# Eight subtractions of expert weights, six of them on GpSimd and two on VectorE, all placed on VectorE behind the early list

## Chip, cores and metric

The kernel runs on one core of one Trainium2 chip. The metric is the device time of one execution in microseconds (us); lower is better.

## What is computed

A layer of attention without a score matrix, a norm, a layer of experts and a second norm, on 4 sequences of 1024 tokens with 512 features, in fp32. The parts that matter here:

```python
x_prev = shift x by one token
k, v, r = (x_prev + (x - x_prev) * tm) @ W.T + b        # three mixes, three matrices
wkv = _wkv_scan(k, v, time_decay, time_first)           # running maximum, two weighted sums, their quotient
out = (sigmoid(r) * wkv) @ Wo.T + bo
x = _layernorm(x + out)
logits = xt @ wg
probs = softmax(logits); idx = argmax(probs)            # one expert of 8 for each token
expert_out = xt @ W[e].T + b[e]                         # only the chosen one counts
x = _layernorm(x + gate * expert_out)
```

## The kernel before

Products of fp32 operands are made of fp32r parts: each operand is rounded to a high part, and the remainder is the low part; a product is high x high + high x low + low x high. For the weights of the experts ScalarE rounds (`expert_hi`, line 957, into `w_e_hi`), and the low part `w_e_lo` is the subtraction `w_e_raw - w_e_hi`, written over the raw weights. Each of the 8 experts is 4 pieces of 128x512.

The work has two stages. The first goes over 8 blocks (4 sequences, 2 halves of 512 tokens), each in 4 chunks of 128 features: TensorE projects k, v and r (line 511), VectorE runs the recurrence (three scans and their products), GpSimd adds the entering state to the sums (`leave`, lines 1093 and 1095), ScalarE does exponentials. The output projection (line 529), the first norm and the logits of a block follow one or two blocks later. The rows go to `x1_rows` in HBM.

The second stage is the experts. Tokens are sorted by expert, in tiles of 128 rows. Of the first 24 row tiles an early list is made while the last block is still under way; from it come 17 full tiles (`FULL`), each of one expert. The rest, with the last 8 row tiles, makes 22 mixed tiles. For each tile GpSimd gathers rows by an indirect DMA (`gather`, line 1174), TensorE turns them (line 680) and multiplies (`expert`, line 689), VectorE adds bias and residual (lines 1719 and 1726), ScalarE normalizes (`norm2`, lines 1041 to 1047), and GpSimd scatters the rows to the output (line 1181). Six tiles are in flight.

The order of each engine is written out by hand; engines meet by semaphores alone. On VectorE, behind the last block's recurrence, stand in this order: the rows of the block before (`add_rows`, line 1319, with `statistics`, line 1329, and `aggregate`, line 1333), the columns of the early list (`early_columns`, lines 1574 to 1579), their split (`split_dest`), the matrices of tiles and slots (`place_tiles`, lines 1506 and 1508, `place_slots`, line 1501), the experts of the full tiles (`tile_experts`, lines 1512 to 1519, with `tiles_ready`), the first row tile of the last block (`add_last` and `shift_last`, lines 1524 to 1531), the ids (line 1643, with `ids_ready`), and the other three row tiles, with the subtractions of experts 6 and 7 (line 1539) between them. TensorE multiplies the slot and tile matrices into the list (`list_full`, line 662, `listed`).

On GpSimd, `expert_lo` (line 1157) subtracts experts 0 to 5 in four pieces each; it stands ahead of the first gather, and expert 0 ahead of the last chunk's `leave`. The counter `we_split` is raised once for each expert, in the order of the experts:

```python
part.then_inc(we_split, 1)                       # GpSimd, experts 0 to 5
dve.wait_ge(we_split, e)                         # VectorE, experts 6 and 7: in order behind GpSimd's
pe.wait_ge(we_split, e + 1)                      # TensorE, ahead of a full tile of expert e
pe.wait_ge(we_split, EXPERTS)                    # TensorE, ahead of the mixed tiles
pool.wait_ge(ids_ready, 1)                       # GpSimd, ahead of the first gather
pool.wait_ge(gate_stored[0], 16)
pe.wait_ge(turned_lo, k + 1)                     # TensorE, ahead of tile k: VectorE's split_gathered(k)
pe.wait_ge(y_taken, k + (TILES + 1))             # and VectorE's additions up to add_gathered(k - 2)
```

Of the kernel before, what the change touches and what calls it, by code (L numbers as in the profile page):

```python
# [31 lines left out]
ALU = mybir.AluOpType  # L32
ACT = mybir.ActivationFunctionType
AX_X = mybir.AxisListType.X
F32 = mybir.dt.float32
# [26 lines left out]
PART = 8  # L62
BIAS_RING = 3
AHEAD = 5
POOL_EXPERTS = 6
ROW = H + 16
EPS = 1e-5
EXPONENT_CAP = 27.0
# [35 lines left out]
def build(nc, x, xT, w_square, w_experts, vectors, bo, b_experts, wg, out):  # L104
    x1_rows = nc.dram_tensor("x1_rows", [TOKENS + 1, ROW], F32, kind="Internal").ap()

    with ExitStack() as ctx:
# [251 lines left out]
        def home(e):  # L359

            return (e + EXPERTS - 2) % EXPERTS
# [718 lines left out]
        def _(pool):  # L1080
# [6 lines left out]
            def leave(i, c):  # L1087

                g = i * CH + c
                p, b = c // 2, c % 2  # L1090
                pool.wait_ge(b_scanned, g + 1)
                pool.wait_ge(evn_ready, g + 1)
                pool.tensor_tensor(ee[:, p, b, :], ee[:, p, b, :], state[:, b, SB, 0:TB], ALU.add).then_inc(den_added, 1)  # L1093
                pool.wait_ge(a_scanned, g + 1)
                pool.tensor_tensor(evn[:, p, b, :], evn[:, p, b, :], state[:, b, SA, 0:TB], ALU.add).then_inc(num_added, 1)
# [54 lines left out]
            walk(pool, step, pool.Fori)  # L1150


            def expert_lo(e):
                pool.wait_ge(we_hi, e + 1)
                p = home(e)
                for c in range(CH):
                    part = pool.tensor_tensor(w_e_lo[:, p, c], w_e_raw[:, p, c], w_e_hi[:, p, c].bitcast(F32), ALU.subtract)  # L1157
                part.then_inc(we_split, 1)

            last = BLOCKS - 1  # L1160
            mix_lo(last, R, 0)
            mix_lo(last, R, 1)
            for c in range(CH - 1):
                leave(last, c)
            expert_lo(0)
            leave(last, CH - 1)
            for e in range(1, POOL_EXPERTS):
                expert_lo(e)

            def gather(k):  # L1170
                if k >= RING:
# [38 lines left out]
        def _(dve):  # L1210
# [310 lines left out]
            def add_last(j):  # L1521
                dve.wait_ge(last_loaded, TPB * 16)
                dve.wait_ge(y_filled, last * TPB + (j + 1))
                dve.tensor_tensor(rows_last[:, j], rows_last[:, j], last_banks[j], ALU.add).then_inc(y_taken, 1)
                dve.wait_ge(y_taken, last * TPB + (j + 3))
                dve.bn_stats(bn[:, j, :], rows_last[:, j]).then_inc(bn_done, 1)
                aggregate(last, j)
# [6 lines left out]
            def expert_lo(e):  # L1534

                p = home(e)
                dve.wait_ge(we_split, e)
                dve.wait_ge(we_hi, e + 1)
                dve.tensor_tensor(w_e_lo[:, p], w_e_raw[:, p], w_e_hi[:, p].bitcast(F32), ALU.subtract).then_inc(we_split, 1)

# [92 lines left out]
            place_tiles(place_k, 0, EARLY, COLS)  # L1633
            for n in range(EARLY // PART):
                place_slots(place_early[n], n * PART, PART)
            tile_experts(FULL, taken[:, 1:], iota_row, after_full, expert_full, slot_full)
            link(dve.tensor_tensor(left_end[:], ranked[:, 1, :], taken[:], ALU.subtract))
            link(dve.tensor_tensor(n_left[:], counts[:, 0, 1:], n_taken[:], ALU.subtract))
            add_last(0)
            shift_last(0)  # L1640
            dve.wait_ge(listed, 1)
            dve.tensor_copy(left_row[:], lists_ps[:, FULL:FULL + LEFT])
            dve.tensor_scalar(ids_full[:, :, 0], lists_ps[:, 0:FULL], -1.0, None, ALU.add).then_inc(ids_ready, 1)
            add_last(1)
            shift_last(1)
            expert_lo(6)
            add_last(2)
            shift_last(2)

            def choose_late():  # L1650
                largest(EARLY, LATE, late_ps, lg2)
# [91 lines left out]
            split_gathered(0, 0)  # L1743
            add_last(3)
            split_gathered(1, 1)
            shift_last(3)
            expert_lo(7)
            add_bias(0, 0, 0)
            add_bias(1, 0, 1)
# [76 lines left out]
```

## Time and profile before

| | |
|---|---|
| median of 3 runs | 684.97 us |
| the runs | 684.97, 684.98, 683.03 us |
| the profiled execution | 683.71 us |
| its span | 681.7 us |
| mean granted TensorE clock | 0.947 of full speed |
| VectorE busy | 565.0 us |
| TensorE busy | 591.1 us |
| GpSimd busy | 319.4 us |

The time of a run covers a little more than the span, which goes from the first to the last instruction of the profiled execution: 2.0 us here. Times below are counted from the span's start. PE is TensorE, DVE is VectorE, ACT is ScalarE, POOL is GpSimd, SPq the queue of SyncE's transfers. In brackets stands how long the engine was idle before the instruction and what ended the wait.

### The profile page before, as it was taken

Reading aid. Unit: us, or ns where it says so; the run is one execution under the profiler, and the core shown is the slowest. Engines: PE = TensorE matmul, PEld = TensorE weight load, DVE = VectorE, ACT = ScalarE, POOL = GpSimd, SP = SyncE. Lnnn points to the kernel's source line nnn. Section 1 sums busy time; section 2 is a strip of 40 time slices with the busy share of each in tenths; the row PEclk is TensorE's granted clock in tenths of the full one; section 3 lists DMA queues with packets and bytes.
Section 4 is the critical chain, followed back from the end, with each engine's and each line's share of the span. In section 5 each row is a group of like instructions: output and inputs, shape, how many; then the busy total and the mean of one; then the engine's idle time right before and its main releaser. Section 6 shows DMA issues by size and latency. Waiting matters only on the chain. (4 is left out here: it accounts for less than half of the span.)

```text
span 681.7 us, 8970 instructions
## 1 busy us (share of the span) xinstructions
PE 591.1 (87%) x2484; PEld 435.7 (64%) x2485; DVE 565.0 (83%) x873; ACT 403.0 (59%) x735; POOL 319.4 (47%) x237
## 2 busy tenths in 40 slices
PE   0676779999999999999999999987669779899992
PEld 0464666676677777668668668743448657677771
DVE  7959898999999999999999899799866658576661
ACT  3356475487477567766756756543446446587763
POOL 4744545444443551552462453276841435456541
PEclk9779898999999999999999999898779879899996
DMA  8030010032032022003104106246153566757650
GB/s 306 5 123 1 0 62 0 1 108 63 15 104 67 16 78 76 31 32 122 31 4 151 32 0 232 91 171 197 62 187 80 159 189 188 206 178 220 210 163 6
DMA packets 36565, 67.63 MB, mean 99 GB/s; under 512 B 8560, under 2 KB 8560, under 8 KB 36532
## 3 DMA queue, kind: packets, MB, share of 16 engines
q1 hardware_dynamic: 30292, 48.29, 22.5%
q0 software_dynamic: 6240, 18.94, 8.8%
q8 instruction: 16, 0.26, 0.2%
q14 instruction: 17, 0.14, 0.1%
HBM read 50.17 MB, written 18.88 MB: 101 GB/s over the span
## 5 line engine op out<-in xcount | busy, mean ns | idle before, releaser
L1083 POOL TENSOR_TENSOR mixed<-unsplit,mixed 128x1024 fp32r<-128x1024 f32 x44 | 104.4, 2395 | 133.8 <-ACT mixed L762 133.8
L511 PE MATMUL kb<-mixed,w_kvr 128*128 128x512 f32 x384 | 99.6, 410 | 23.8 <-DVE mixed L1437 16.9
L689 PE MATMUL y_ps<-w_e_hi,xgT 128*128 x312 | 111.0, 418 | 7.3 <-issue 5.2
L511 PE MATMUL vb<-mixed,w_kvr 128*128 128x512 f32 x384 | 102.8, 419 | 14.4 <-DVE evn L1275 8.9
L511 PE MATMUL rb<-mixed,w_kvr 128*128 128x512 f32 x384 | 101.8, 415 | 5.7 <-DVE ee L1289 4.7
L511 PEld LDWEIGHTS kb<-mixed,w_kvr 128*128 128x128 f32 x384 | 74.7, 198 | 42.6 <-issue 16.5
L529 PE MATMUL y_ps<-w_o,rw 128*128 128x512 f32 x224 | 100.7, 592 | 0.0
L511 PEld LDWEIGHTS vb<-mixed,w_kvr 128*128 128x128 f32 x384 | 74.5, 198 | 36.1 <-DVE evn L1275 11.7
L511 PEld LDWEIGHTS rb<-mixed,w_kvr 128*128 128x128 f32 x384 | 73.4, 193 | 27.8 <-DVE ee L1289 5.9
L1226 DVE SCALAR_TENSOR_TENSOR unsplit<-diff,vec,xb 128x512 f32<-128x512 f32 x96 | 74.2, 833 | 8.1 <-PE kb L511 6.1
L1093 POOL TENSOR_TENSOR ee<-ee,state 128x512 f32<-128x512 f32 x32 | 34.9, 1092 | 96.2 <-DVE state L1259 95.5
L689 PEld LDWEIGHTS y_ps<-w_e_hi,xgT 128*128 128x128 f32 x312 | 61.2, 196 | 24.3 <-issue 11.3
L529 PEld LDWEIGHTS y_ps<-w_o,rw 128*128 128x128 f32 x224 | 42.5, 190 | 42.3 <-issue 40.4
L777 ACT ACTIVATE e<-state 128x512 f32<-128x512 f32 x32 | 20.2, 630 | 75.6 <-DVE state L1243 75.6
L689 PE MATMUL y_ps<-w_e_lo,xgT 128*128 x156 | 63.6, 408 | 0.0
L762 ACT ACTIVATE mixed<-unsplit 128x1024 fp32r<-128x1024 f32 x48 | 50.5, 1054 | 19.2 <-DVE unsplit L1226 19.2
L1726 DVE SCALAR_TENSOR_TENSOR yo<-y_ps,xg,yo 128x512 f32<-128x512 f32 x39 | 29.2, 750 | 35.6 <-PE y_ps L689 21.9
L1157 POOL TENSOR_TENSOR w_e_lo<-w_e_raw,w_e_hi 128x512 fp32r<-128x512 f32 x24 | 38.0, 1614 | 14.1 <-ACT w_e_hi L957 14.1
L1181 POOL DMA_INDIRECT out<-yo,ids_full x17 | 18.1, 1065 | 49.7 <-ACT yo L1047 27.5
L1259 DVE TENSOR_TENSOR_SCAN state<-eb,state,e 128x512 f32<-128x512 f32 x32 | 40.8, 1274 | 0.4 <-ACT state L812 0.4
L1047 ACT ACTIVATE yo<-yo,nmr,rstd 128x512 f32<-128x512 f32 x39 | 31.8, 816 | 15.2 <-DVE nmr L1733 12.2
L1236 DVE TENSOR_TENSOR_SCAN state<-kb,state,wdec 128x512 f32<-128x512 f32 x32 | 40.3, 1259 | 0.0
(227 smaller groups left out, 1104.6 us busy)
## 6 DMA issues: line engine op xcount, KB each, us to landing
bias<-b_experts SPq DMA_DIRECT2D x39, 256.0 KB
w_e_raw<-w_experts SPq DMA_DIRECT2D x8, 1024.0 KB, 8.2
rows<-x SPq DMA_DIRECT2D x28, 256.0 KB, 2.6
x_rows<-rows SPq DMA_DIRECT2D x28, 256.0 KB, 2.1
xb<-xT SPq DMA_DIRECT2D x4, 1026.0 KB, 5.3
xb<-xT SPq DMA_DIRECT2D x3, 1024.0 KB, 5.1
w_raw<-w_square SPq DMA_DIRECT2D x2, 1024.0 KB, 10.4
xb<-xT SPq DMA_DIRECT2D x2, 512.0 KB, 5.3
```

Source lines behind the costliest of these rows:

```text
L511: mm = pe.matmul(bank, w_kvr[m][:, a, h, o:o + P], mixed[m][:, bb, h, :], start=(k == 0), stop=(k == 3 * CH - 1))
L529: mm = pe.matmul(y_ps[:, j % 2, :], rw[:, half, c, j * P:(j + 1) * P], w_o[:, c, :], start=False, stop=(c == CH - 1))
L689: mm = pe.matmul(y_ps[:, n % 2, :], xgT[n % 3][:, a, c, :], w[:, bass.ds(p, 1), c, :].rearrange("p u o -> p (u o)"), start=(c == 0 and (a, ...
L762: act.activation(mixed[m][:, HI, 2 * hp:2 * hp + 2, :], unsplit[m][:, LO, 2 * hp:2 * hp + 2, :], ACT.Copy).then_inc(mixed_hi, 1)
L1047: act.activation(yo[n][:], yo[n][:], ACT.Identity, bias=nmr2[:, n:n + 1], scale=rstd2[:, n:n + 1]).then_inc(out_ready, 1)
L1083: pool.tensor_tensor(mixed[m][:, LO, 2 * hp:2 * hp + 2, :], unsplit[m][:, LO, 2 * hp:2 * hp + 2, :], mixed[m][:, HI, 2 * hp:2 * hp + 2, :] ...
L1093: pool.tensor_tensor(ee[:, p, b, :], ee[:, p, b, :], state[:, b, SB, 0:TB], ALU.add).then_inc(den_added, 1)
L1157: part = pool.tensor_tensor(w_e_lo[:, p, c], w_e_raw[:, p, c], w_e_hi[:, p, c].bitcast(F32), ALU.subtract)
L1226: ins = dve.scalar_tensor_tensor(out=unsplit[m][:, LO, h, :], in0=diff[:, h, :], scalar=vec[:, VEC_MK + m, h:h + 1], in1=xb[:, h, 0:TB], o ...
L1236: dve.tensor_tensor_scan(state[:, c % 2, SQ, 1:], kb[:], wdec[:, c:c + 1].to_broadcast([P, TB]), state[:, c % 2, SQ, 0:1], ALU.max, ALU.ad ...
L1259: dve.tensor_tensor_scan(state[:, c % 2, SB, 1:], eb[:], e2[:, c % 2], state[:, c % 2, SB, 0:1], ALU.mult, ALU.add).then_inc(b_scanned, 1)
L1726: dve.scalar_tensor_tensor(out=yo[n][:], in0=y_ps[:, n % 2, :], scalar=gate_of(n), in1=yo[n][:], op0=ALU.mult, op1=ALU.add, accum_out=sum2 ...
```

## The change

GpSimd subtracts no expert any more. VectorE subtracts all eight, each in one operation on 128x2048, and no longer waits for the counter of the expert before. Expert 0 stands ahead of the ids, behind the first row tile; experts 1 to 4 between and behind the row tiles 1 and 2; experts 5 to 7 around the fourth row tile. The operations of `tile_experts` move from ahead of the first row tile to behind the ids.

```diff
--- before.py
+++ after.py
@@ -62,7 +62,6 @@
 PART = 8
 BIAS_RING = 3
 AHEAD = 5
-POOL_EXPERTS = 6
 ROW = H + 16
 EPS = 1e-5
 EXPONENT_CAP = 27.0
@@ -1150,22 +1149,11 @@
             walk(pool, step, pool.Fori)
 
 
-            def expert_lo(e):
-                pool.wait_ge(we_hi, e + 1)
-                p = home(e)
-                for c in range(CH):
-                    part = pool.tensor_tensor(w_e_lo[:, p, c], w_e_raw[:, p, c], w_e_hi[:, p, c].bitcast(F32), ALU.subtract)
-                part.then_inc(we_split, 1)
-
             last = BLOCKS - 1
             mix_lo(last, R, 0)
             mix_lo(last, R, 1)
-            for c in range(CH - 1):
+            for c in range(CH):
                 leave(last, c)
-            expert_lo(0)
-            leave(last, CH - 1)
-            for e in range(1, POOL_EXPERTS):
-                expert_lo(e)
 
             def gather(k):
                 if k >= RING:
@@ -1534,7 +1522,6 @@
             def expert_lo(e):
 
                 p = home(e)
-                dve.wait_ge(we_split, e)
                 dve.wait_ge(we_hi, e + 1)
                 dve.tensor_tensor(w_e_lo[:, p], w_e_raw[:, p], w_e_hi[:, p].bitcast(F32), ALU.subtract).then_inc(we_split, 1)
 
@@ -1633,19 +1620,23 @@
             place_tiles(place_k, 0, EARLY, COLS)
             for n in range(EARLY // PART):
                 place_slots(place_early[n], n * PART, PART)
-            tile_experts(FULL, taken[:, 1:], iota_row, after_full, expert_full, slot_full)
+            add_last(0)
+            shift_last(0)
+            expert_lo(0)
             link(dve.tensor_tensor(left_end[:], ranked[:, 1, :], taken[:], ALU.subtract))
             link(dve.tensor_tensor(n_left[:], counts[:, 0, 1:], n_taken[:], ALU.subtract))
-            add_last(0)
-            shift_last(0)
             dve.wait_ge(listed, 1)
             dve.tensor_copy(left_row[:], lists_ps[:, FULL:FULL + LEFT])
             dve.tensor_scalar(ids_full[:, :, 0], lists_ps[:, 0:FULL], -1.0, None, ALU.add).then_inc(ids_ready, 1)
+            tile_experts(FULL, taken[:, 1:], iota_row, after_full, expert_full, slot_full)
             add_last(1)
+            expert_lo(1)
             shift_last(1)
-            expert_lo(6)
             add_last(2)
+            expert_lo(2)
             shift_last(2)
+            expert_lo(3)
+            expert_lo(4)
 
             def choose_late():
                 largest(EARLY, LATE, late_ps, lg2)
@@ -1743,7 +1734,9 @@
             split_gathered(0, 0)
             add_last(3)
             split_gathered(1, 1)
+            expert_lo(5)
             shift_last(3)
+            expert_lo(6)
             expert_lo(7)
             add_bias(0, 0, 0)
             add_bias(1, 0, 1)
```

VectorE from the slot matrices to the ids; before, from the fourth of the seven operations of `tile_experts` on (`place_early` are the slot matrices, `rows_last` the last block's row tiles, `ids_full` the list that the gathers read):

```order
L1515 TENSOR_SCALAR moved_e<-tile_e 128x17
L1516 SCALAR_TENSOR_TENSOR moved_e<-tile_e,moved_e 128x17
L1518 CAST expert_full<-tile_e 128x17
L1519 CAST slot_full<-moved_e 128x17
L1637 TENSOR_TENSOR left_end<-ranked,taken 128x9
L1638 TENSOR_TENSOR n_left<-counts,n_taken 128x8
L1524 TENSOR_TENSOR rows_last<-rows_last,rb 128x512
L1526 BN_STATS bn<-rows_last 128x6
L1333 BN_AGGR stats<-bn 128x2
L1531 SCALAR_TENSOR_TENSOR nmr<-stats,rstd 128x1
L1642 COPY left_row<-lists_ps 128x14
L1643 TENSOR_SCALAR ids_full<-lists_ps 128x17
```

and in the change, from the last slot matrix on:

```order
L1489 TENSOR_TENSOR place_early_127<-slot_q,iota_q 128x1024
L1512 TENSOR_TENSOR rows_last<-rows_last,rb 128x512
L1514 BN_STATS bn<-rows_last 128x6
L1321 BN_AGGR stats<-bn 128x2
L1519 SCALAR_TENSOR_TENSOR nmr<-stats,rstd 128x1
L1526 TENSOR_TENSOR w_e_lo<-w_e_raw,w_e_hi 128x2048
L1626 TENSOR_TENSOR left_end<-ranked,taken 128x9
L1627 TENSOR_TENSOR n_left<-counts,n_taken 128x8
L1629 COPY left_row<-lists_ps 128x14
L1630 TENSOR_SCALAR ids_full<-lists_ps 128x17
L1500 TENSOR_TENSOR after_full<-iota_row,taken 128x136
```

The seven operations from `after_full` to `slot_full` no longer stand between the slots and the ids; a subtraction of `w_e_lo` does.

VectorE from the second row tile (`rows_last<-rows_last,vb`) to the splits of the gathered tiles 0 and 1 (`xgT`), before:

```order
L1524 TENSOR_TENSOR rows_last<-rows_last,vb 128x512
L1526 BN_STATS bn<-rows_last 128x6
L1333 BN_AGGR stats<-bn 128x2
L1531 SCALAR_TENSOR_TENSOR nmr<-stats,rstd 128x1
L1539 TENSOR_TENSOR w_e_lo<-w_e_raw,w_e_hi 128x2048
L1524 TENSOR_TENSOR rows_last<-rows_last,y_ps 128x512
L1526 BN_STATS bn<-rows_last 128x6
L1333 BN_AGGR stats<-bn 128x2
L1531 SCALAR_TENSOR_TENSOR nmr<-stats,rstd 128x1
L1710 TENSOR_TENSOR xgT_129<-kb,xgT_129 128x512
L1524 TENSOR_TENSOR rows_last<-rows_last,y_ps 128x512
```

and in the change:

```order
L1512 TENSOR_TENSOR rows_last<-rows_last,vb 128x512
L1514 BN_STATS bn<-rows_last 128x6
L1321 BN_AGGR stats<-bn 128x2
L1526 TENSOR_TENSOR w_e_lo<-w_e_raw,w_e_hi 128x2048
L1519 SCALAR_TENSOR_TENSOR nmr<-stats,rstd 128x1
L1512 TENSOR_TENSOR rows_last<-rows_last,y_ps 128x512
L1514 BN_STATS bn<-rows_last 128x6
L1321 BN_AGGR stats<-bn 128x2
L1526 TENSOR_TENSOR w_e_lo<-w_e_raw,w_e_hi 128x2048
L1519 SCALAR_TENSOR_TENSOR nmr<-stats,rstd 128x1
L1526 TENSOR_TENSOR w_e_lo<-w_e_raw,w_e_hi 128x2048 x2
L1701 TENSOR_TENSOR xgT_129<-kb,xgT_129 128x512
```

One subtraction (expert 6) stood between the second row tile and the split of tile 0; four stand there now (experts 1 to 4).

GpSimd from the last chunks of the recurrence (`ee`, `evn`) to the first gathers, before:

```order
L1157 TENSOR_TENSOR w_e_lo<-w_e_raw,w_e_hi 128x512 x4
L1093 TENSOR_TENSOR ee<-ee,state 128x512
L1095 TENSOR_TENSOR evn<-evn,state 128x512
L1157 TENSOR_TENSOR w_e_lo<-w_e_raw,w_e_hi 128x512 x20
L1174 DMA xg<-x_rows,ids_full 128x528 x6
```

and in the change:

```order
L1092 TENSOR_TENSOR ee<-ee,state 128x512
L1094 TENSOR_TENSOR evn<-evn,state 128x512
L1092 TENSOR_TENSOR ee<-ee,state 128x512
L1094 TENSOR_TENSOR evn<-evn,state 128x512
L1162 DMA xg<-x_rows,ids_full 128x528 x6
```

Nothing stands between the last `leave` and the gathers any more.

## Rows read from the trace of the kernel before

**Rows 1.** The page: busy time of each engine with its share of the span.

```profile
PE 591.1 (87%) x2484; PEld 435.7 (64%) x2485; DVE 565.0 (83%) x873; ACT 403.0 (59%) x735; POOL 319.4 (47%) x237
```

**Rows 2.** Timeline of GpSimd (POOL), 440 to 535 us: start, length, engine, line, operation.

```profile
463.08 11.70 POOL L1157 TENSOR_TENSOR w_e_lo<-w_e_raw,w_e_hi 128x512 fp32r<-128x512 f32 x8 [4.93 <-ACT w_e_hi L957]
479.67 14.35 POOL L1157 TENSOR_TENSOR w_e_lo<-w_e_raw,w_e_hi 128x512 fp32r<-128x512 f32 x8 [4.89 <-ACT w_e_hi L957]
497.84 1.15 POOL L1174 DMA_INDIRECT xg<-x_rows,ids_full  x1 [3.82 <-DVE ids_full L1643]
...
500.56 2.32 POOL L1174 DMA_INDIRECT xg<-x_rows,ids_full  x1 [0.30 <-issue]
...
526.74 0.98 POOL L1174 DMA_INDIRECT xg<-x_rows,ids_full  x1 [0.30 <-issue]
```

**Rows 3.** Timeline of VectorE, 454 to 502 us.

```profile
454.55 1.19 DVE L1560 TENSOR_SCALAR counts_i<-counts_i 128x18 int32<-128x18 int32 x1
...
462.50 1.23 DVE L1302 SCALAR_TENSOR_TENSOR er<-ee,er 128x1024 f32<-128x1024 f32 x1
463.76 2.18 DVE L1312 SCALAR_TENSOR_TENSOR rw<-evn,er 128x1024 f32<-128x1024 f32 x1
...
469.71 1.26 DVE L1574 TENSOR_TENSOR beyond<-work_early,n_taken 128x192 f32<-128x192 f32 x1
...
473.69 1.30 DVE L1577 TENSOR_TENSOR work_early<-work_early,beyond 128x192 f32<-128x192 f32 x1
475.03 0.36 DVE L1578 TENSOR_TENSOR work_early<-work_early,hot_early 128x192 f32<-128x192 f32 x1
...
480.12 0.83 DVE L1324 SCALAR_TENSOR_TENSOR nmr<-stats,rstd 128x2 f32<-128x2 f32 x1 [2.94 <-ACT rstd L840]
...
481.85 1.91 DVE L1508 TENSOR_TENSOR place_k<-place_k,token 128x768 fp32r<-128x768 f32 x1
...
490.32 1.35 DVE L1512 TENSOR_TENSOR after_full<-iota_row,taken 128x136 f32<-128x136 f32 x1
...
494.99 0.69 DVE L1524 TENSOR_TENSOR rows_last<-rows_last,rb 128x512 f32<-128x512 f32 x1
...
497.38 0.17 DVE L1643 TENSOR_SCALAR ids_full<-lists_ps 128x17 uint32<-128x17 f32 x1
...
499.76 2.29 DVE L1539 TENSOR_TENSOR w_e_lo<-w_e_raw,w_e_hi 128x2048 fp32r<-128x2048 f32 x1
```

**Rows 4.** Line 1501 by form: shortest, median, longest ns, first and last start.

```profile
L1501 DVE TENSOR_TENSOR place_early<-slot_q,iota_q x3: 2284/2289/2293, 483.7 to 488.1; 128x1024 fp32r<-128x1024 f32 x3
L1501 DVE TENSOR_TENSOR place_late<-slot_q,iota_q x1: 1216/1216/1216, 562.9 to 562.9; 128x1024 fp32r<-128x1024 f32 x1
```

**Rows 5.** Busy time of engines, granted clock, DMA share and GB/s in three stretches.

```profile
440.00:497.00 57.00, 41.92 (x131) 23.97 (x129) 51.96 (x72) 24.83 (x30) 40.29 (x26) 0.88 0.44 149
533.80:538.30 4.50, 4.47 (x14) 3.56 (x14) 1.01 (x3) 1.61 (x6) 1.50 (x2) 0.62 0.50 165
538.80:541.70 2.90, 2.90 (x16) 2.31 (x14) 2.73 (x9) 1.80 (x5) 0.00 (x0) 1.00 0.35 95
```

**Rows 6.** Timeline of TensorE, 455 to 535 us.

```profile
459.68 0.47 PE L517 MATMUL y_ps<-bo,ones 128*128 128x512 f32 x1 [1.03 <-DVE rows L1319]
459.98 3.60 PE L529 MATMUL y_ps<-w_o,rw 128*128 128x512 f32 x8
...
511.45 0.50 PE L689 MATMUL y_ps<-w_e_hi,xgT 128*128 x1 [1.28 <-issue]
...
521.43 0.47 PE L689 MATMUL y_ps<-w_e_hi,xgT 128*128 x1
...
531.96 0.66 PE L680 MATMUL kb<-ident,xg 128*128 128x128 f32 x4 [2.53 <-DMA xg<-x_rows,ids_full]
```

**Rows 7.** Timeline of ScalarE, 477 us.

```profile
477.70 1.89 ACT L957 ACTIVATE w_e_hi<-w_e_raw 128x2048 fp32r<-128x2048 f32 x1
```

**Rows 8.** Timeline of the SyncE queue, 477 us: its transfers.

```profile
477.11 5.75 SPq L393 DMA_DIRECT2D x_rows<-rows  x4
```

## Prediction

> **What bounds the kernel now.** I read the page first: VectorE is busy 83% of the span and TensorE 87% [rows 1], means over stages with different limits. The chain that ended last shows only the closing transfer, so the bound near the change has to be read from the timelines of 440 to 535 us, engine by engine, GpSimd's first. It holds 24 list subtractions (four to an expert, experts 0 to 5); the last ended at 479.67 + 14.35 = 494.02, and the first gather of rows starts at 497.84, behind the write of `ids_full` by VectorE, which ends at 497.55 [rows 2, 3]. So GpSimd was not late. What its work costs is seen on VectorE: with GpSimd in a subtraction, an operation on 128x192 takes 1.30 us; GpSimd stops at 463.08 + 11.70 = 474.78, and the next one of the same size takes 0.36 [rows 2, 3]. An 18-element operation takes 1.19; a 1024-element product takes 2.18 where the refinement of the same size before it, with GpSimd idle, took 1.23; the three slot matrices take 2.29 each, the same form alone 1.22 [rows 3, 4]. And VectorE has no slack there: it is busy for 52.0 of the 57 us from 440 to 497 [rows 5]. VectorE sets the time of the list, and GpSimd slows VectorE: that is what the change touches.
>
> From the ids to the first expert tile it is TensorE that sets the time now, working in order through logits, the last output projection and turned rows; tile 0 starts at 511.45, tile 2 at 521.43 [rows 6].
>
> **The change, part by part.** All times are places in the profiled execution; I follow the same chain through the new order.
>
> *1. GpSimd's pieces are gone, up to the end of the slots.* Before 466 us the relief is partly lost. The refinement and the product at 442 to 447 would give back 1.0 each, but the gate behind them waits for ScalarE, and some 0.3 is left. Four 1.19 us operations of the counts fall to about 0.2 (4 us), the product at 463.76 from 2.18 to 1.23; TensorE binds instead. The last projection of the block before starts at 459.68 behind a wait of 1.03 us for VectorE and ends at 459.98 + 3.60 = 463.58 [rows 6]; without that wait and 0.3 earlier it ends at 462.3. One addition, four statistics and four aggregates follow (3.3 us at 0.6, 0.6 and 0.08 each, none of them slowed now): the columns of the list start at 465.6 and not at 469.71 [rows 3]. **Gain 4.1.**
> The columns: four operations of 1.30 fall to 0.36, **3.8.** Then VectorE waits 2.94 us for ScalarE's deviation, which stands behind a rounding of 1.89 [rows 3, 7]. ScalarE's inputs come earlier by the same 7.9 us, so I keep the wait. Behind it the shift falls from 0.83 to 0.16, the tile product from 1.91 to 0.95 (three quarters of the 1.22 form), and the slot matrices from a pitch of 2.2 to 1.14 (their length less the 0.08 by which such operations overlap): **4.8.** The slots are complete 12.7 us earlier, at 477.7; TensorE's listing ends 2 us behind them and hides behind the next item.
>
> *2. The order up to the ids.* Now 7.2 us lie between slots and ids (490.32 to 497.55): seven operations of the tile numbers and two small ones to 494.99, row tile 0 with its shift, the ids [rows 3]. Then: row tile and shift 2.4, one subtraction 2.2 (2.29 less the overlap), the two small ones 0.4, the ids 0.3, together 5.3; the tile numbers come behind. **Gain 2.0** after rounding. The ids are ready at 482.8, 14.7 earlier. The gathers also need the stored rows of the block before; those stores start at 477.11 [rows 8] behind ScalarE's norm, so they move up by 4 to 8 us and don't bind.
>
> *3. From the ids to tile 0.* Now 511.45 - 497.55 = 13.9 us, set by TensorE. Then VectorE is the long way: tile numbers 1.6 (seven at some 0.2, GpSimd idle), row tile 1 1.6, subtraction 1 2.2, a shift 0.1, row tile 2 1.6, subtraction 2 2.2, a shift 0.1, subtractions 3 and 4 4.4, and only then the split of gathered tile 0, 0.7: 14.5 us, to 497.3. TensorE turns tile 2 (0.6), passes the gap of 1.28 that stands there now [rows 6] and starts tile 0 at 499.2, 16.4 us behind the ids. **Loss 2.4**, so tile 0 is 12.3 us earlier. TensorE's own way, through the norm of row tile 2, brings it to the turns by about 495.4, so it is covered. Of the other subtractions none is waited for: number 5 ends at 501.5, 6 and 7 at 506; the addition behind them, which tile 2 needs, ends at 508.6, and tile 2 is due at 509.2 (521.43 - 511.45 behind tile 0). That cover is 0.6 us thin.
>
> *4. TensorE's clock.* The granted clock is 0.62 from 533.80 to 538.30, the tile behind a wait of 2.53 us for a gather, and 1.00 in the next; the two take 4.5 and 2.9 us [rows 5, 6]. Tile 0 now comes right behind the last projection and the turns, and is fast. In the new order TensorE idles some two us before turn 2, and more before that, so I take a slow tile 0: **loss 1.6.** Bounds: nothing if the clock is up, 3.2 if two tiles are slow.
>
> *5. Behind tile 2* I move the stage rigidly. The first scatter hangs on TensorE's turns of the last rows and ScalarE behind them, gather 6 (526.74) on that scatter, and turn 6 waits for it at 531.96 [rows 2, 6]. The loop has the same members in the same order in both kernels.
>
> Sum: 4.1 + 3.8 + 4.8 + 2.0 - 2.4 - 1.6 = 10.7 us. The profiled execution took 683.71 (span 681.7 and 2.0 around it), which gives 673.0. The median of the runs shown is 684.97, 1.26 above that execution, with one run of three below it; I add half a microsecond: **673.5.**
>
> The relief's bounds: 0, if the operations keep their length, and about 18, if every slowed one of the stretch counted. I take 12.7, since rows of equal shape beside each other carry it and only what others bind is taken off.
>
> **The rivals.**
> *A, the forecast:* a gain of 8.5 to 13 (675.2 to 670.7). For it: equal shapes at 1.30 and 0.36 us with only GpSimd's stop between them.
> *B, more:* the clock is up and VectorE gets to the split as early as the ids allow: the whole 14.7 reaches the end, 669.0. Against it: four subtractions stand ahead of the split in VectorE's order.
> *C, gathers and subtractions collide.* The six gathers now start at 483 and fall on subtractions 1 and 2. In the kernel before the third gather takes 2.32 us where the one at 526.74 takes 0.98; it starts 0.8 us into the subtraction at 499.76 [rows 2, 3]. A late gather costs nothing: three times 1.4 more puts the start of the sixth at 494, and with 5.2 us to landing (526.74 to 531.96) it is there ahead of its tile. But if the gather goes first and VectorE stands for it, six times 0.98 = 5.9 lie on the long way of item 3, and 4.8 of the gain is left: 678.9. Against: the subtraction at 499.76 beside the gathers kept its 2.29.
> The Trainium skill, SBUF — State Buffer, section "Who interferes with whom", says that a tensor operation on two tensors has no two-port mode and takes only the shared read interface, from which it infers that it does not hold up descriptor generation on GpSimd; by that page C would not occur and its chance would go to A. The 2.32 us gather speaks against that inference, so I keep C.
> *D, slower:* the relief does not come, because the long VectorE operations are due to the transfers of the weights or the rows and not to GpSimd. Then item 2's 2.0 us stand against 2.4 + 1.6 of items 3 and 4, in front of tile 0: 2.0 us slower, 685.7. It decides from a relief below 2.0 us, where I count 12.7. Against it: 1.22 for the form at 562.9 and 0.36 at 475.03 [rows 3, 4]. That the change doesn't do what it says is no case: the order of both engines shows it.
>
> **How the numbers follow.** A 0.60; B 0.15; C and other partial losses, a gain of 2 to 8.5 us, 0.18; an end within 0.3% (2 us), about what a measurement of this kernel can tell from no change, 0.03; D 0.04. The low end is B less half a microsecond, 668.5; the high end is C, 679.0. Faster 0.93, same 0.03, slower 0.04.
>
> **What would show it.** Right: slot matrices of 1.2 us, column operations near 0.36, the write of the ids near 482.7 and GpSimd's first gather 0.3 behind it; VectorE without a gap from there to the split of tile 0 near 497; tile 0 near 499 at a granted clock of about 0.6, tile 2 near 510.5; and from tile 2 to the end 160 us as now. Wrong: slot matrices still above 2 us (D); subtractions 1 and 2 longer than 3 us (C); tile 0 before 498 or at full clock (B); or a distance from tile 2 to the end that differs by over 2 us, which none of the items holds.

## The result, and the profile after

The changed kernel takes 665.79 us (median of 4 runs, 664.97 to 667.01), the kernel before in the same session 684.98 (683.03 to 685.92). The ratio is 0.9725, 95% interval 0.9699 to 0.9751: 19 us, 2.8% faster. The forecast was 673.5 with a range down to 668.5; the direction was right, and the gain is two thirds larger than forecast and outside the range.

The profiled execution took 664.97 us with a span of 663.0, against 683.71 and 681.7: 18.7 us less. Span and busy times on the page of the changed kernel (before: [rows 1]):

```profile
span 663.0 us, 8951 instructions
...
PE 583.5 (88%) x2484; PEld 431.0 (65%) x2485; DVE 559.8 (84%) x879; ACT 403.1 (61%) x735; POOL 281.2 (42%) x213
```

VectorE does 13.6 us more subtraction and is busy 5.2 us less, so its other operations are 18.8 us shorter together. Where the 18.7 us lie is read by comparing the same instructions. VectorE, from the columns of the list to the first addition of the experts (answers to [rows 3]):

```profile
464.93 0.32 DVE L1561 TENSOR_TENSOR beyond<-work_early,n_taken 128x192 f32<-128x192 f32 x1
...
466.07 0.36 DVE L1564 TENSOR_TENSOR work_early<-work_early,beyond 128x192 f32<-128x192 f32 x1
...
466.47 0.36 DVE L1565 TENSOR_TENSOR work_early<-work_early,hot_early 128x192 f32<-128x192 f32 x1
...
471.55 0.16 DVE L1312 SCALAR_TENSOR_TENSOR nmr<-stats,rstd 128x2 f32<-128x2 f32 x1 [2.94 <-ACT rstd L839]
...
473.49 3.49 DVE L1489 TENSOR_TENSOR place_early<-slot_q,iota_q 128x1024 fp32r<-128x1024 f32 x3
...
481.88 0.17 DVE L1630 TENSOR_SCALAR ids_full<-lists_ps 128x17 uint32<-128x17 f32 x1
...
495.56 0.68 DVE L1701 TENSOR_TENSOR xgT<-kb,xgT 128x512 fp32r<-128x512 f32 x1
...
506.88 0.74 DVE L1717 SCALAR_TENSOR_TENSOR yo<-y_ps,xg,yo 128x512 f32<-128x512 f32 x1
```

The column operation at 466.07 takes 0.36 as the one behind it (before 1.30 and 0.36); the three slot matrices take 3.49 together and not 6.71; the ids are written at 481.88, 15.5 us earlier than 497.38. TensorE, the starts of tiles 0, 1 and 2 and the turn of tile 6 (answers to [rows 6]):

```profile
498.26 0.79 PE L688 MATMUL y_ps<-w_e_hi,xgT 128*128 x1 [0.78 <-issue]
...
504.03 0.48 PE L688 MATMUL y_ps<-w_e_hi,xgT 128*128 x1
...
509.88 0.47 PE L688 MATMUL y_ps<-w_e_hi,xgT 128*128 x1
...
519.08 0.66 PE L679 MATMUL kb<-ident,xg 128*128 128x128 f32 x4 [1.20 <-DMA xg<-x_rows,ids_full]
```

Tile 2 starts 11.55 us earlier than at 521.43. From there to the end of the span it is 153.1 us where it was 160.3: **7.1 us of the gain lie behind tile 2**, where I had moved everything rigidly. GpSimd, two of the first six gathers, the first scatter and gather 6 (answers to [rows 2]):

```profile
486.30 1.90 POOL L1162 DMA_INDIRECT xg<-x_rows,ids_full  x1 [0.30 <-issue]
...
489.76 2.24 POOL L1162 DMA_INDIRECT xg<-x_rows,ids_full  x1 [0.30 <-issue]
...
513.55 1.03 POOL L1169 DMA_INDIRECT out<-yo,ids_full  x1 [21.55 <-ACT yo L1046]
...
514.88 0.98 POOL L1162 DMA_INDIRECT xg<-x_rows,ids_full  x1 [0.30 <-issue]
```

| step of the forecast | forecast | measured |
|---|---|---|
| 0: anything ahead of 440 us | 0 | 0.5 |
| 1: start of the columns | 4.1 | 4.3 (469.71 to 464.93, less 0.5) |
| 1: columns | 3.8 | 3.8 |
| 1: shift, tile and slot matrices | 4.8 | 4.9 (slots complete at 476.89, before 490.32) |
| 2: slots to ids | 2.0 | 2.1 (5.2 us, before 7.2) |
| 3: ids to tile 0 | -2.4 | -2.3 (16.2 us, before 13.9) |
| 4: slow clock in tile 0 | -1.6 | -1.6 (tile 0 to 1: 5.77, before 4.13) |
| 5: tile 2 to the end | 0 | 7.1 |

(The difference of the sum to 18.7 is rounding.) The start of every tile of the second stage, from TensorE's timelines of both kernels (first product of each), shows where the 7.1 us arise:

```
tile           before            after       earlier by
2              521.43            509.88      11.6
3              526.39  +4.96     514.84 +4.96   11.6
4              533.83  +7.44     520.80 +5.96   13.0
5              538.82  +4.99     524.86 +4.06   14.0
8              553.67  +8.37     536.84 +5.52   16.8
9              558.91  +5.24     541.37 +4.53   17.5
12             570.92  +4.68     551.93 +3.24   19.0
17             591.29  +5.97     572.77 +5.79   18.5
36             659.72            641.08         18.6
```

(+ is the distance from the tile before.) TensorE turns the rows of gather 6 ahead of tile 4 and those of gather 10 ahead of tile 8, where it waited 3.42 us before and 0.61 now. So the delays go round with the ring: 2.4 us are gained at tiles 4 and 5, 3.5 at 8 and 9, 1.5 up to 12, and 0.4 is lost later. Tile 4 of the kernel before ran at a granted clock of 0.62 [rows 5]; now:

```profile
521.00:524.00 3.00, 3.00 (x16) 2.46 (x16) 1.00 (x4) 1.53 (x5) 0.85 (x2) 1.00 0.80 269
```

The granted clock (behind the busy times) is 1.00. TensorE waited 1.20 us for gather 6, before 2.53 [rows 6].

### The profile page after: what moved, and what is told of

It is laid out like the page before. It is cut to its first block and busy times, and to the rows that moved or that the text cites. A ratio compares the mean times of both kernels' runs of the same rounds, so it can differ in the third digit from the quotient of the medians.

```text
span 663.0 us, 8951 instructions
## 1 busy us (share of the span) xinstructions
PE 583.5 (88%) x2484; PEld 431.0 (65%) x2485; DVE 559.8 (84%) x879; ACT 403.1 (61%) x735; POOL 281.2 (42%) x213
## 5 line engine op out<-in xcount | busy, mean ns | idle before, releaser
L688 PE MATMUL y_ps<-w_e_hi,xgT 128*128 x312 | 109.6, 414 | 7.8 <-issue 6.0
L510 PEld LDWEIGHTS kb<-mixed,w_kvr 128*128 128x128 f32 x384 | 73.9, 196 | 44.1 <-issue 16.2
L1254 DVE TENSOR_TENSOR_SCAN state<-eb,state,ev 128x512 f32<-128x512 f32 x32 | 40.3, 1258 | 0.0
L1094 POOL TENSOR_TENSOR evn<-evn,state 128x512 f32<-128x512 f32 x32 | 38.0, 1188 | 2.5
```

The costliest lines, as they stand in the source:

```text
L510: mm = pe.matmul(bank, w_kvr[m][:, a, h, o:o + P], mixed[m][:, bb, h, :], start=(k == 0), stop=(k == 3 * CH - 1))
L688: mm = pe.matmul(y_ps[:, n % 2, :], xgT[n % 3][:, a, c, :], w[:, bass.ds(p, 1), c, :].rearrange("p u o -> p (u o)"), start=(c == 0 and (a, ...
L1254: dve.tensor_tensor_scan(state[:, c % 2, SA, 1:], eb[:], ev2[:], state[:, c % 2, SA, 0:1], ALU.mult, ALU.add).then_inc(a_scanned, 1)
```

## Experiments

The theory of the first part, GpSimd's subtractions block VectorE, is tested by leaving them out (1) and by undoing the reorder (2, 9). For the 7.1 us I formed **theory R**: in the kernel before, the packets of the bias load of tile 6 go ahead of those of gather 6, the gather is a microsecond late, TensorE idles long enough to fall to its slow level, and the delay goes round the ring of six tiles. Its rival N says that the stretch is shorter for another reason. Behind R stood the question why gather 6 comes sooner at all, **theory L** below. Of each run I read the time, tile 2, and the rest from tile 2 to the end of the span. One profile stands for each kernel, and it need not be a run at the median. Every kernel ran four or more times with the kernel before between; the ratios are against that.

**1. b_no_pool.** GpSimd's 24 subtractions left out; the products that took `w_e_lo` take `w_e_hi` in its place, so their number stays.

```diff
-                for c in range(CH):
-                    part = pool.tensor_tensor(w_e_lo[:, p, c], w_e_raw[:, p, c], w_e_hi[:, p, c].bitcast(F32), ALU.subtract)
-                part.then_inc(we_split, 1)
+                pool.sem_inc(we_split, 1)
...
-                    for a, w in ((HI, w_e_hi), (HI, w_e_lo), (LO, w_e_hi)):
+                    for i, a in enumerate((HI, HI, LO)):
...
```

> The kernel before without GpSimd's 24 list subtractions: w_e_lo of experts 0 to 5 is not made, and the expert products read w_e_hi in its place (same count and shape of matmuls). Relief alone, with the order of before. Theory (the long VectorE operations are GpSimd's doing): slot matrices 1.2 us, ids about 15.5 us earlier (12.7 of relief and 2.7 in the tile numbers), TensorE's way behind the ids as before, tile 0 about 15 us earlier than 511.45, tile 2 about 15 us earlier than 521.43. Rival (other cause): slot matrices stay at 2.3 us and tile 0 within 1 us of 511.45. From tile 2 to the end: 160 us if that stretch is shortened only by something else in the change, about 153 if the change's 7 us there come with an earlier or differently timed start of the stage or with GpSimd's absence.

Measured: 665.82 us, ratio 0.9742 (0.9686 to 0.9798). VectorE:

```profile
475.44 3.49 DVE L1499 TENSOR_TENSOR place_early<-slot_q,iota_q 128x1024 fp32r<-128x1024 f32 x3
...
483.22 0.17 DVE L1641 TENSOR_SCALAR ids_full<-lists_ps 128x17 uint32<-128x17 f32 x1
```

The slot matrices take 3.49 us and the ids come at 483.22, 14.2 earlier, so the cause of the long operations is shown. Tile 0 starts at 498.32 and tile 2 at 509.77: 13.1 and 11.7 earlier, not 15, because the columns start at 466.88 here and not at 464.93 as in the change (the blocks ahead ended 2 us later in this profile), and because tile 0 is slow here too. Counted from the columns, tile 0 is 41.7 us behind in the kernel before, 33.3 in the change and 31.4 here: the six subtractions cost 1.9 us on VectorE (four of them stand ahead of the split of tile 0, 8.8 us of work that TensorE's own way mostly covers; two stand behind it), and their absence from GpSimd gives 10.3 in this stretch. The order of `tile_experts` is no part of the 1.9: with it put back in the change (9) the stretch is 33.3 too. The time is that of the change within the intervals. The rest from tile 2 is 155.9.

**2. b_tiles_behind.** In the kernel before, `tile_experts` behind the ids and nothing else.

```diff
-            tile_experts(FULL, taken[:, 1:], iota_row, after_full, expert_full, slot_full)
             link(dve.tensor_tensor(left_end[:], ranked[:, 1, :], taken[:], ALU.subtract))
...
             dve.tensor_scalar(ids_full[:, :, 0], lists_ps[:, 0:FULL], -1.0, None, ALU.add).then_inc(ids_ready, 1)
+            tile_experts(FULL, taken[:, 1:], iota_row, after_full, expert_full, slot_full)
```

> The kernel before with tile_experts moved behind the ids and nothing else. Theory: the ids come at about 493.3 instead of 497.55 (4.3 earlier), the gathers must wait for GpSimd's last subtraction (494.0), row tile 0 comes 4.3 earlier and with it TensorE's way to tile 0, but row tile 1 behind the tile numbers (which cost 4 us under GpSimd, 1.6 when it stops) comes only some 2 us earlier, so tile 0 is about 2 us earlier and the run 680 to 683 us, if tile 2 to the end stays 160. Rival: the reorder carries much of the 19 us: below 678.

Measured: 683.28 us, ratio 0.9998 (0.9967 to 1.0028); the ids come 2.5 us earlier and not 4.3, tile 0 starts at 509.61, 1.8 earlier, as expected, but runs at a granted clock of 0.72 instead of 1.00, and tile 2 at 520.98, 0.45 earlier. The reorder alone is worth nothing that can be measured.

**3. b_bias6_late.** In the kernel before, the bias load of tile 6 waits for one more addition.

```diff
-                    sp.wait_ge(bias_added, k + 1 - BIAS_RING)
+                    sp.wait_ge(bias_added, k + 1 - BIAS_RING + (1 if k == 6 else 0))
```

> The kernel before, SyncE waits for one more addition (bias_added 5 instead of 4) ahead of the bias load of tile 6, so that the load is issued at about 528.5 instead of 527.44, behind gather 6 (526.74) in the transfer queues. Theory R (rhythm: gather 6 loses a microsecond to that load, TensorE idles long enough to fall to the slow clock, and the delays go round the ring of six tiles): turn 6 earlier by about 1 us, tile 4 at full clock, tile 2 to the end 153 to 156 us, time 678 to 681. Theory N (the 7 us behind tile 2 have nothing to do with it): tile 2 to the end stays 160, time 684 to 686.

Measured: 679.24 us (10 runs, 675.17 to 682.94), ratio 0.9940 (0.9911 to 0.9969). TensorE, turn 6 and tile 4:

```profile
529.88 0.66 PE L680 MATMUL kb<-ident,xg 128*128 128x128 f32 x4 [0.74 <-DMA xg<-x_rows,ids_full]
...
531.50 0.50 PE L689 MATMUL y_ps<-w_e_hi,xgT 128*128 x1 [0.96 <-issue]
```

Turn 6 waits 0.74 us instead of 2.53, tile 4 comes 5.38 behind tile 3 (7.44), tile 5 4.12 behind tile 4 (4.99), tile 8 5.79 (8.37). The rest from tile 2 is 151.9 in this profile. One wait of one load, which takes nothing away, gives this profile a rest even below that of the change (153.1). But it is the fastest of the ten runs: in the median the edit gives 4 us.

**4. a_gather6_late.** In the changed kernel, twelve small memsets on GpSimd ahead of gather 6.

```diff
+        spare = place("spare", [P, 48], F32)
...
+                    if k + AHEAD == RING:
+                        for q in range(12):
+                            pool.memset(spare[:, 4 * q:4 * q + 4], 0.0)
                     gather(k + AHEAD)
```

> The changed kernel with twelve small memsets on GpSimd ahead of gather 6, which comes about 0.5 us later and so behind the bias load of tile 6. Theory R: turn 6 waits about 1 to 1.5 us longer, tile 4 falls to the slow clock, tile 2 to the end 157 to 160 us instead of 153, time 669 to 672. Theory N: at most the 0.5 us, time 665.5 to 666.5.

Measured: 670.38 us, ratio 0.9826 (0.9776 to 0.9876). Gather 6 starts at 515.48, 5.31 behind tile 2, as in the kernel before (526.74 - 521.43) and not 5.00 as in the change. TensorE, and the clock in tile 4:

```profile
520.52 0.65 PE L680 MATMUL kb<-ident,xg 128*128 128x128 f32 x4 [2.37 <-DMA xg<-x_rows,ids_full]
```

```profile
523.00:527.00 4.00, 4.00 (x14) 3.16 (x12) 0.34 (x2) 1.03 (x3) 1.67 (x2) 0.61 0.55 174
```

The wait is 2.37, the clock 0.61, tile 4 comes 7.32 behind tile 3 and tile 5 4.99 behind tile 4, tile 8 8.11, within 0.3 of the kernel before. The rest is 158.4. **A delay of 0.3 us at one gather costs 4.6 us** between the medians.

The first link of R can be read in the packets that the traces recorded, in all fourteen profiles. In four of them the load is issued 0.54 to 0.71 us behind the start of gather 6 (before, 2, 4, 5): the load's first packet starts 1.51 to 1.69 us behind the gather's start, and the gather's own packets only from 2.58 to 2.70 on. In the ten others the load is issued 0.85 us or more behind, and the gather's packets start at 1.67 to 1.69, ahead of the load's. With the load ahead, turn 6 waits 2.37 to 2.57 us, and the rest is 158.4 to 160.2. With the gather ahead, the wait is 0.74 to 1.94, but the rest is 151.9 to 157.8, and more in 11 and 12. So the order costs the gather a microsecond, as R says; it does not alone set the rest.

**5. a_pool_filler.** Why is gather 6 0.3 us sooner? It follows the first scatter directly, and that follows ScalarE's write of tile 0. ScalarE and GpSimd in the kernel before:

```profile
523.41 0.82 ACT L1047 ACTIVATE yo<-yo,nmr,rstd 128x512 f32<-128x512 f32 x1 [0.23 <-DVE nmr L1733]
```

```profile
525.40 1.03 POOL L1181 DMA_INDIRECT out<-yo,ids_full  x1 [18.77 <-issue]
```

and in the change:

```profile
511.86 0.82 ACT L1046 ACTIVATE yo<-yo,nmr,rstd 128x512 f32<-128x512 f32 x1 [0.23 <-DVE nmr L1724]
```

(its scatter stands above, at 513.55). The write ends at 524.23 and 512.68, and the scatter starts 1.17 and 0.87 us behind. The gap was 1.17 in the three kernels with the 24 subtractions (before, 2, 3) and 0.87 without (the change, 1). Theory L: the length of GpSimd's program does it. So the changed kernel got 24 memsets of 128x2 where the subtractions had been:

```diff
+        spare = place("spare", [P, 48], F32)
...
             for c in range(CH):
                 leave(last, c)
+            for q in range(24):
+                pool.memset(spare[:, 2 * q:2 * q + 2], 0.0)
```

> The changed kernel with 24 memsets of 128x2 on GpSimd (0.1 us each) where the 24 subtractions stood, so that GpSimd's program has the length of the kernel before. Theory L (the length of GpSimd's program sets how soon its first scatter follows ScalarE: 1.17 us in the kernels with the 24 subtractions, 0.87 without): the gap is 1.17 again, gather 6 is behind the bias load, turn 6 waits about 2.5 us, tile 2 to the end 158 to 160, time 670 to 673. Rival W (the gap comes from something else, such as the work before): gap 0.87, tile 2 to the end 153, time 665 to 667.

Measured: 672.99 us, ratio 0.9818 (0.9769 to 0.9868). ScalarE, GpSimd, TensorE:

```profile
513.65 0.82 ACT L1047 ACTIVATE yo<-yo,nmr,rstd 128x512 f32<-128x512 f32 x1 [0.23 <-DVE nmr L1727]
```

```profile
515.65 1.02 POOL L1172 DMA_INDIRECT out<-yo,ids_full  x1 [22.05 <-issue]
```

```profile
522.22 0.66 PE L680 MATMUL kb<-ident,xg 128*128 128x128 f32 x4 [2.57 <-DMA xg<-x_rows,ids_full]
```

The gap is 1.18, turn 6 waits 2.57, the distances of tiles 4, 5 and 8 are 7.55, 5.00 and 8.21, the rest 159.3. Memsets that are done 60 us earlier and that nobody waits for come with 6.2 us more behind tile 2. The medians lie 7.2 apart, but 1.6 us of the distance between the profiles arose before 443 us, ahead of the memsets (454.06 to 454.85).

**6. b_pool_whole.** The converse, with all the work left in: GpSimd's subtractions as 6 operations and not 24.

```diff
-                for c in range(CH):
-                    part = pool.tensor_tensor(w_e_lo[:, p, c], w_e_raw[:, p, c], w_e_hi[:, p, c].bitcast(F32), ALU.subtract)
-                part.then_inc(we_split, 1)
+                pool.tensor_tensor(w_e_lo[:, p], w_e_raw[:, p], w_e_hi[:, p].bitcast(F32), ALU.subtract).then_inc(we_split, 1)
```

> The kernel before with GpSimd's subtractions as 6 operations of 128x2048 instead of 24 of 128x512: the same work in a program that is 18 instructions shorter. Theory L: the first scatter follows ScalarE by 0.87 us instead of 1.17, gather 6 is ahead of the bias load, turn 6 waits 1.2 instead of 2.5, tile 2 to the end 153 to 156 us. The list may move by a few us either way, since a whole subtraction blocks VectorE for longer at a time. Rival (the gap depends on having the subtractions, not on their number): 1.17, tile 2 to the end 160.

Measured: 684.57 us, ratio 0.9989 (0.9950 to 1.0028).

```profile
526.33 0.82 ACT L1047 ACTIVATE yo<-yo,nmr,rstd 128x512 f32<-128x512 f32 x1 [0.23 <-DVE nmr L1731]
```

```profile
528.01 1.02 POOL L1179 DMA_INDIRECT out<-yo,ids_full  x1 [18.56 <-ACT yo L1047]
```

```profile
442.18 5.47 DVE L1300 SCALAR_TENSOR_TENSOR er<-ee,er 128x1024 f32<-128x1024 f32 x1
...
465.97 5.40 DVE L1310 SCALAR_TENSOR_TENSOR rw<-evn,er 128x1024 f32<-128x1024 f32 x1
...
482.26 4.07 DVE L1322 SCALAR_TENSOR_TENSOR nmr<-stats,rstd 128x2 f32<-128x2 f32 x1 [2.94 <-ACT rstd L840]
```

The gap is 0.86, so it hangs on the number of instructions and not on the work. Turn 6 waits 1.68 and tile 4 keeps the full clock (tile 5 3.82 behind it); the rest is 157.8, 2.4 us less than before but above the 153 to 156 expected. VectorE pays it back ahead of the list: the refinement and the product take 5.47 and 5.40 us beside a whole subtraction (2.21 and 2.18 beside pieces), so the columns start 5.4 later, at 475.15. From there to tile 0 it is 39.2 us, 2.5 less than before, although a shift on 128x2 takes 4.07 and not 0.83. Tile 2 comes 2.9 later.

**7. a_lo0_in_gap.** In the changed kernel, the subtraction of expert 0 in VectorE's wait for ScalarE.

```diff
             split_dest(0, EARLY)
+            expert_lo(0)
             shift(before, 1)
...
             shift_last(0)
-            expert_lo(0)
```

> The changed kernel with the subtraction of expert 0 moved from ahead of the ids into the 2.94 us in which VectorE waits for ScalarE's deviation. Theory: the subtraction (2.2) is free there, the ids come 2.2 earlier, VectorE is the long way to tile 0, so tile 0 and the end come 2.2 earlier: 663.0 to 664.5. Rival (TensorE is the long way): ids 2.2 earlier, but tile 0 less than 1 earlier, 665 to 666.

Measured: 669.09 us, ratio 0.9773 (0.9724 to 0.9822), profiled execution 668.08. The wait took the subtraction, but the ids come only 1.3 us earlier and not 2.2: the columns start 0.5 later in this profile, and VectorE waits 0.56 for TensorE's listing ahead of the ids. The ids are written at 480.63, tile 0 starts at 497.11, 1.2 earlier, and tile 2 at 508.36, 1.5 earlier. Behind it:

```profile
518.28 0.66 PE L679 MATMUL kb<-ident,xg 128*128 128x128 f32 x4 [1.94 <-issue]
```

```profile
521.00:524.00 3.00, 3.00 (x9) 2.34 (x8) 0.51 (x2) 0.96 (x2) 0.80 (x1) 0.52 0.47 168
```

Gather 6 is 4.99 behind tile 2 as in the change, and so is the bias load, but the turn waits 1.94 us and the clock falls to 0.52: distances 6.61, 4.98, 8.41, the rest 157.8. What ended the wait the trace doesn't say. Work moved into a wait made the kernel no faster, and its median is above the change's. R as I had put it, by the order of the two transfers alone, doesn't cover this one.

**8. a_bias6_late.** The load held back as in 3, in the changed kernel (same edit).

> The changed kernel with the bias load of tile 6 held back by one addition. Gather 6 is ahead of that load already, so theory R expects nothing: 665 to 666.5, fewer runs above 666.5. Rival: the load also slows gather 7 or a tile waits for its bias; over 667 or below 664.

Measured: 668.35 us (665.21 to 669.34), ratio 0.9760 (0.9727 to 0.9794). The profile is that of the change (tile 4 5.82 behind tile 3, rest 152.7, span 663.2), but this is the fastest of five runs, and the other four took 668.31 to 669.34. The median missed the expectation by 2 us and lies where the rival had put it (over 667); whether by the rival's cause, the profile of the fastest run can't show. The load held back brings nothing here, where gather 6 is ahead already.

**9. a_tiles_first.** The reorder undone in the changed kernel: `tile_experts` directly behind `place_slots` (the edit of 2 in reverse).

> The changed kernel with tile_experts back ahead of the first row tile, the reorder undone. Theory: the ids come 1.6 us later, but the seven operations leave VectorE's way behind the ids, so the split of tile 0 and tile 0 stay within 0.3 us; 665 to 668. Rival (the reorder carries 2 us or more of the gain): tile 0 over 1.5 us later, over 668.

Measured: 669.70 us (666.85 to 670.74), ratio 0.9780 (0.9728 to 0.9831). The ids come 1.8 later (483.67), tile 0 at 498.42, 0.16 later, as expected; the rest is 154.4 in the profile. The median is above what was expected and in the rival's range (over 668), but tile 0 speaks against the rival's cause. The profile is that of the fastest of the four runs, so where the median's 2.9 us more lie is not settled.

**10. a_gate_late.** The store of the late gates behind the bias load of tile 11.

```diff
-                if k == 8:
+                if k == 11:
                     sp.wait_ge(gate_ready, 2)
```

> The changed kernel with the store of the late gates (64 KB in pieces of 64 bytes) behind the bias load of tile 11 instead of tile 8, so that gathers 10 and 11 don't meet it. Theory: turn 10 comes earlier, the distance from tile 7 to tile 8 falls from 5.52 towards 3.3 to 4, 1 to 2 us of gain at tile 9 and part of it at the end, 663.5 to 666. Rival (turn 10 waits for its scatter and ScalarE, not for the transfers): the distance stays 5.5, or the store meets a later gather and gives it back, 665 to 668.

Measured: 665.82 us, ratio 0.9742 (0.9677 to 0.9806). Tile 8 comes 6.12 us behind tile 7, not the 3.3 to 4 expected and not the 5.52 of the change; tile 9 follows 3.25 behind it (4.53), so from tile 7 to tile 9 it is 9.37 and not 10.05. Tile 12 is 4.65 behind tile 11 and not 3.24, and the rest is 152.7. What is gained at tile 9 is given back at tile 12, as the rival had it; the expected effect on turn 10 did not come.

**11, 12. a_spread and a_safe**, meant to be faster: the subtractions in VectorE's waits. In the first:

```diff
             split_dest(0, EARLY)
+            expert_lo(0)
             shift(before, 1)
...
             shift_last(0)
-            expert_lo(0)
...
             add_last(1)
-            expert_lo(1)
             shift_last(1)
             add_last(2)
-            expert_lo(2)
             shift_last(2)
-            expert_lo(3)
-            expert_lo(4)
+            expert_lo(1)
+            expert_lo(2)
...
+                for e in {0: (4, 5), 2: (6,), 3: (7,)}.get(k, ()):
+                    expert_lo(e)
                 shift2(k, n)
...
             split_gathered(1, 1)
-            expert_lo(5)
             shift_last(3)
-            expert_lo(6)
-            expert_lo(7)
+            expert_lo(3)
```

with the edit of 3. This order is valid only for routings in which no early tile needs a late expert. The second keeps all subtractions ahead of the first addition: expert 0 behind the product of 444 us, 1 ahead of `shift(before, 1)`, 2 and 3 behind `shift_last(2)`, 4 behind `split_gathered(1, 1)`, 5 to 7 behind the first two `add_bias`.

> A version meant to be faster: expert 0 in the gap, 1 and 2 directly ahead of the split of tile 0 (behind the shifts that ScalarE and TensorE wait for), 3 behind the fourth row tile, 4 to 7 in VectorE's waits within the first four steps of the tiles, bias load of tile 6 held back. Theory: VectorE is no longer the long way; TensorE is, with 14.9 us from the ids to tile 0 as in b_no_pool instead of 16.2, ids 2.2 earlier: tile 0 3.5 earlier than 498.26, time 661.5 to 663.5. Rival: the subtractions within the steps delay additions that TensorE waits for, over 665.

> A version meant to be faster for any routing (all eight subtractions ahead of the first addition): expert 0 at VectorE's wait of 1.6 us behind the product, expert 1 in the wait of 2.9, 2 and 3 ahead of the split of tile 0, 4 behind the splits, 5 to 7 behind the split of tile 2 and the first bias additions. Theory: tile 0 at about 494.5, tile 2 at 505.5 to 506.5 (held by the first addition), 4 us ahead of 509.88; if the rhythm stays fast, 661.5 to 663.5. Rival: the rhythm turns slow (turn 6 waits 2 us or more) and gives 3 to 5 us back: 665 to 668.

Measured: a_spread 665.60 us, ratio 0.9709 (0.9673 to 0.9746); a_safe 665.94, ratio 0.9706 (0.9649 to 0.9763). a_spread starts tile 0 at 493.38, 4.9 earlier than the change, and is 5.9 ahead at tile 8, and 1.4 us behind at tile 18: the rest is 160.5. Gather 7 takes 2.76 us beside a subtraction:

```profile
511.49 2.76 POOL L1162 DMA_INDIRECT xg<-x_rows,ids_full  x1 [0.31 <-issue]
```

a_safe has tile 0 at 496.64, but its first addition comes late and tile 2 at 509.91, and turns slow behind it (tile 8 8.83 behind tile 7); this profile is the slowest of its four runs. Both medians missed the 661.5 to 663.5 expected and lie in the rivals' ranges. Neither is told from the change by its interval: I have no version that beats it.

## Why the prediction was wrong

Items 1 to 4 held, each within 0.5 us. The relief was GpSimd's: rows of equal shape, one under GpSimd's subtraction and one beside it, forecast it rightly, and experiment 1 shows the cause. The bounds others set ahead of 466 us, the 2.94 us wait for ScalarE that stayed, VectorE's long way from the ids to the split of tile 0 without a gap, and the slow tile 0 all came as written. The six subtractions, 2.2 us each and four of them ahead of tile 0, cost 1.9 us together, since TensorE's way to tile 0 covers the rest.

The step that failed is **item 5, "Behind tile 2 I move the stage rigidly"**, because "the loop has the same members in the same order in both kernels". It has, but the rows that I cited there were of a disturbed round: gather 6, 5.2 us from its start to its landing, a wait of 2.53 and a tile at 0.62 of the clock behind it. I took that wait for a property of the loop, and the 160.3 us behind tile 2 became 153.1. It hangs on whose packets go first, the gather's or the bias load's, and 0.3 us at one gather decide that (4, 5). The change got the gather ahead by an effect that nobody reads in the diff: GpSimd's program was 24 instructions shorter, and with 24 others in their place the load went first again and the rest was 159.3 and not 153.1 (5). Taking 18 away had put the gather ahead as well (6). No rival held it; B, which allowed more, put it at the clock of tile 0 and the ids. The chance that the stage behind a moved start runs otherwise should have stood in the range with some 7 us at its fast end: the row in question (wait, then slow tile) was in my own item 4 as the price of an idle TensorE.

Rival C (gathers and subtractions collide) came half true: gathers 3 and 5 took 1.90 and 2.24 us beside subtractions (0.95 the one between), and the subtractions kept 2.26. By the Trainium skill, SBUF — State Buffer, "Who interferes with whom", a two-tensor operation should not hold up descriptor generation; the rows of the change and of a_spread (2.76) speak against that inference again. It cost nothing here, since tile 0 came as forecast; what it cost in a_spread no run shows by itself. Rival D is refuted by experiment 1.

Of the 18.7 us between the profiles, 0.5 arose ahead of 440 us, 11.1 by the mechanism forecast, and 7.1 by the rhythm. That split belongs to these two profiles: the rest from tile 2 is 151.9 to 157.8 us in eight profiles that all have gather 6 ahead (1, 3, 6 to 10, the change), and the medians of 8 and 9 lie 2.6 and 3.9 us above that of the change. So the gather's order is shown, and how much of the 7.1 us is its share is not. How an earlier start, the order of the transfers and TensorE's granted clock act together is open; experiment 7, with gather and load as in the change and still a wait of 1.94 us and a rest of 157.8, shows that the order is not all of it. Why a program with more instructions makes GpSimd's first scatter 0.3 us later was not tried beyond 5 and 6.

## What to carry to other kernels

Look at what an idle-looking engine does to its neighbour before counting its work as free: here work that GpSimd finished in time cost VectorE, which set the pace, 10 us, while the same work done by VectorE itself cost 2. When a change moves the start of a ring of gathers and scatters, don't carry its length over from one profile: look for waits behind which the granted clock falls, and for transfers issued within a microsecond of each other, and widen the range by what the ring can lose or win (here some 7 us). And test such a ring by a small delay in either direction (a held load, a few memsets) before crediting the edit with the gain.

## What was unexpected of the hardware

- GpSimd's first scatter starts 0.87 us behind ScalarE's write, or 1.17 when GpSimd's program holds 24 more instructions ahead of it, be they subtractions or memsets (24 of them take 0.79 us) done 60 us earlier; with 6 large subtractions it is 0.86.
- A delay of 0.3 us at one gather of 39 costs 4.6 us (670.38 against 665.79). A load issued 0.55 us behind the gather's start gets its packets ahead, one issued 0.85 behind does not; the wait grows from 1.20 to 2.37 us, the granted clock of the next tile falls from 1.00 to 0.61, and the next gathers come later by that.
- One GpSimd subtraction on 128x2048 makes a VectorE operation on 128x2 last 4.07 us, where one with GpSimd idle takes 0.16; with the subtraction cut in four it was 0.83.
